# Attention scores by query: the spread operand moves from the keys to the queries, one head per matmul

## The reference

```
scores = einsum('bshd,bthd->bhst', q, k) * scale
attn   = softmax(scores + mask, axis=-1)
ctx    = einsum('bhst,bthd->bshd', attn, v)
```

## Time and profile before

| | |
|---|---|
| median of 3 runs | 1446.69 us (1445.44 to 1448.8) |
| span of the profiled execution | 1445.6 us |
| PE busy | 1301.3 us, 12165 matmuls and as many weight loads |
| DVE, POOL, ACT busy | 863.6, 702.4, 571.2 us |
| mean granted clock of PE | 0.961 of full speed |

### The profile page before, as it was taken

How to read it: one execution, slowest core, us unless ns; L and a number is a source line. 1 busy time by engine, 2 the same in 40 slices (tenths; PEclk the granted TensorE clock), 3 DMA queues, 4 the chain that set the end, 5 groups by cost and what they waited for, 6 DMA issues and landing times.

```text
span 1445.6 us, 33878 instructions
## 1 busy us (share of the span) xinstructions
PE 1301.3 (90%) x12165; PEld 1048.3 (73%) x12165; DVE 863.6 (60%) x2071; ACT 571.2 (40%) x1272; POOL 702.4 (49%) x949
## 2 busy tenths in 40 slices
PE   5998889989999999989999999959998999929887
PEld 4666647976777777767899899846766777628776
DVE  3788853337888888736622111258885778773346
ACT  1555545433444555643222222214443455414331
POOL 4566642017777466630233333237785555427426
PEclk9999989998999999979999999979999999959999
DMA  6000000020000000000389998631000000038954
GB/s 255 2 2 0 1 1 30 1 86 17 14 15 5 2 17 15 16 16 1 131 317 325 334 332 316 233 139 31 0 17 9 24 30 22 17 105 303 312 176 145
DMA packets 47371, 137.79 MB, mean 95 GB/s; under 512 B 6926, under 2 KB 29647, under 8 KB 41105
## 3 DMA queue, kind: packets, MB, share of 16 engines
q1 hardware_dynamic: 32944, 110.37, 21.7%
q0 software_dynamic: 7536, 19.67, 4.4%
q10 hardware_dynamic: 6768, 6.16, 1.2%
HBM read 119.54 MB, written 17.56 MB: 95 GB/s over the span
## 4 chain that ended last, share of the span: by engine, by line
PE 70%; DVE 12%; DMA 8%; issue 5%; POOL 3%; ACT 2%; DVEq 0%; SPq 0%; POOLq 0%; ACTq 0%
PE ps L1114 11%; PE ps L981 9%; PE ps L1032 9%; PE ps L1349 8%; PE ps L1076 6%; PE ps L1056 4%; PE ps L1047 4%; PE ps L1361 4%; DMA row_in<-rows_of,from_u 4%; DMA back_of<-w_odd 3%; PE ps L925 2%; PE ps L972 2%; DVE negmax L1791 2%; PE ps L1083 2%; PE ps L1007 2%
## 5 line engine op out<-in xcount | busy, mean ns | idle before, releaser
L1415 ACT ACTIVATE probsT_all<-ps 128x1024 f32<-128x1024 f32 x128 | 131.1, 1025 | 164.0 <-PE ps L981 164.0
L1791 DVE TENSOR_REDUCE negmax<-ps 128x8 f32<-128x1024 f32 x128 | 156.0, 1219 | 59.4 <-PE ps L981 59.2
L1349 PE MATMUL ps<-hT,w_tile 128*128 128x128 f32 x1304 | 161.9, 278 | 0.6 <-ACT act_sb L1673 0.2
L1349 PEld LDWEIGHTS ps<-hT,w_tile 128*128 128x128 f32 x1304 | 153.3, 193 | 3.1 <-issue 0.8
L981 PE MATMUL ps<-qe,kf 32*128 32x256 f32 x1280 | 153.1, 387 | 0.0
L981 PE MATMUL ps<-ke,qf 32*128 32x256 f32 x1024 | 146.0, 403 | 0.0
L759 POOL TENSOR_SCALAR eps_sum<-mv 128x1 f32<-128x1 f32 x112 | 25.5, 228 | 199.1 <-DVE mv L1728 112.2
L981 PEld LDWEIGHTS ps<-qe,kf 32*128 32x128 f32 x1280 | 111.0, 188 | 4.8 <-issue 2.8
L1076 PE MATMUL ps<-probsT_all,va 128*32 128x128 f32 x2560 | 105.4, 283 | 7.6 <-ACT probsT_all L1415 4.4
L2354 DVE TENSOR_TENSOR h_in<-ps,act_sb 128x512 f32<-128x512 f32 x39 | 27.0, 692 | 140.0 <-PE ps L1349 140.0
L700 POOL DMA_INDIRECT back_of<-be,to_u x39 | 39.4, 1010 | 140.4 <-DVE be L2367 140.4
(11 more groups left out here) (288 smaller groups left out, 3350.9 us busy)
## 6 DMA issues: line engine op xcount, KB each, us to landing
w_tile<-in_w_f SPq DMA_DIRECT2D x29, 1536.0 KB, 7.5
w_tile<-in_w_f SPq DMA_DIRECT2D x47, 385.0 KB, 7.0
y_back<-in_w_f SPq DMA_DIRECT2D x10, 1536.0 KB
back_of<-w_odd ACTq DMA_DIRECT2D x47, 128.0 KB, 6.5
ctxT<-in_ctxT SPq DMA_DIRECT2D x32, 128.0 KB, 2.1
rows_of<-nv SPq DMA_DIRECT2D x32, 128.0 KB, 1.7
w_even<-in_w_att SPq DMA_DIRECT2D x3, 1024.0 KB, 7.2
y_back<-back_of SPq DMA_DIRECT2D x6, 512.0 KB, 5.7
```

The costliest lines, as they stand in the source:

```text
L1349: last = mm(ps[:, 2 * which + at.two, fc * P:(fc + 1) * P], w[:, col:col + P], rowT[:, at.two, c, :], start=c == 0, stop=c == KC - 1)
L1415: nc.scalar.activation(half_of(probsT_all, half), ps[:, 2:4].rearrange("p b n -> p (b n)"), ACT.Exp, scale=HD ** -0.5).then_inc(S["probs"], 1)
L1791: nc.vector.tensor_reduce(m, ps[:, 0:2].rearrange("p b (h k) -> p (b h) k", h=HB), AX.X, ALU.max, negate=True).then_inc(S["s_max"], 1)
```

## The change

The spread keys `ke` are dropped. The spread queries `qe`, which `by_key` needs anyway, serve `by_query` too: as stationary operand, one head at a time (128 columns), with the plain keys `kf` as moving operand (128 columns). POOL makes one spread copy for each tile instead of two. `by_query` waits for `qe_sb` where it waited for `ke_sb`, and what waited for `s_out` of two tiles back before it wrote `qf` again (ACT, DVE) waits for `qe_sb` of that tile.

```diff
@@ heads_apart on POOL
                 wait(pool, *(("rotated", tile) if tile.l in ROTARY else ("qk_sb", tile)))
-                wait(pool, "s_out", tile.back(2))
-                apart(ke[:, tile.p], kf[:, tile.q]).then_inc(S["ke_sb"], 1)
                 wait(pool, "st_out", tile.back(4))
                 apart(qe[:, tile.q], qf[:, tile.p]).then_inc(S["qe_sb"], 1)
@@ by_query on PE
-                p, q, last = tile.p, tile.q, tile.back(1)
+                q, last = tile.q, tile.back(1)
                 if half == 0:
-                    wait(pe, "ke_sb", tile)
+                    wait(pe, "qe_sb", tile)
...
-                return [(b, j, qf[:, p], ke[:, p], tile.l == ATT1, "s_out", half) for b, j in enumerate(strips(half, False))]
+                return [(b, j, qe[:, q], kf[:, q], tile.l == ATT1, "s_out", half) for b, j in enumerate(strips(half, False))]
@@ scores on PE
                 for c in range(KC):
-                    for bank, j, a, b, first, name, half in products:
-                        done[name, half] = mm(ps[:, bank, c * D:(c + 1) * D], a[strip(j), c], b[strip(j), c].rearrange("p i k -> p (i k)"),
-                                              start=first, stop=first or c == KC - 1)
+                    for i in range(2):
+                        for bank, j, a, b, first, name, half in products:
+                            if name == "s_out":
+                                at = c * D + i * P
+                                done[name, half] = mm(ps[:, bank, at:at + P], a[strip(j), c, i], b[strip(j), c],
+                                                      start=first, stop=first or c == KC - 1 and i == 1)
+                            elif i == 0:
+                                done[name, half] = mm(ps[:, bank, c * D:(c + 1) * D], a[strip(j), c],
+                                                      b[strip(j), c].rearrange("p i k -> p (i k)"),
+                                                      start=first, stop=first or c == KC - 1)
@@ queries_keys on ACT, before it writes qf and kf
-                    wait(act, "s_out", tile.back(2))
+                    wait(act, "qe_sb", tile.back(2))
@@ rotate on DVE
-                    if tile.l in SOFTMAX:
-                        wait(dve, "s_out", tile.back(2))
+                    wait(dve, "qe_sb", tile.back(2))
```

More of the change, by code:

```diff
@@ L160 @@
         "zmax_sb": (ATT0,), "zero_exp": (ATT0,), "pad_mask": (XATT0,), "pad_in": (XATT0,), "gn_var": (RET,),
-        "gn_eps": (RET,), "gn_rstd": (RET,), "ke_sb": SOFTMAX, "nm_sb": SOFTMAX, "m_out": SOFTMAX, "inj_sb": SOFTMAX,
+        "gn_eps": (RET,), "gn_rstd": (RET,), "nm_sb": SOFTMAX, "m_out": SOFTMAX, "inj_sb": SOFTMAX,
         "o_sb": (RET,), "rotated": ROTARY}
@@ L286, in build @@
             kf = at_attention("kf", [P, 4, KC, P])
-            ke = at_attention("ke", [P, 2, KC, 2, P])
             qe = at_attention("qe", [P, 4, KC, 2, P])
@@ L368, in sem @@
             return S[name]
-        for name in ("var1 rstd1 u_norm var2 rstd2 v_norm base_sb uT_out hT_sb qk_out v_out qk_sb swapped rotated o_sb centred qe_sb ke_sb va_sb "
+        for name in ("var1 rstd1 u_norm var2 rstd2 v_norm base_sb uT_out hT_sb qk_out v_out qk_sb swapped rotated o_sb centred qe_sb va_sb "
                      "s_out s_max st_out probs pv_out nm_sb m_out inj_sb zero_exp o_norm oT_out oT_sb y_out x_done "
```

## The result

The changed kernel takes 1432.76 us (median of 7 runs, 1428.86 to 1441.6) where the kernel before takes 1445.44 us on the same chip (7 runs, 1443.39 to 1448.8). The ratio is 0.9925, interval [0.9896, 0.9954]: faster by 12.7 us in the medians, by 6.6 to 15 us in the interval. The prediction was 1440.8 us, range 1436 to 1448. The three ratios amount to 10.8, 12.5 and 8.4 us.

The account below looks back on a forecast made before the run. PE bounds the kernel, busy nine tenths of the span, with DVE's chain deciding in ATT0. -3.6 - 0.8 + 0.4 - 1.0 - 0.8 - 0.3 + 0.2 = -5.9 us gives span 1439.7, median 1440.8 us; range 1436 to 1448.

Parts of the forecast that it names:

- Rival (a): Query strips in `scores`: narrow pairs outrun the cover of the keys, slower, 1523 us at the upper bound; chance 0.15.
- `s_out` comes 0.03 us later: ATT0: the queries' signal, heading DVE's chain once a step, comes 0.03 us later; 13 steps cost 0.4 us.
- 0.2 in the calls with queries alone: PE in `scores`: the 6 calls without key products end 0.03 us later each, costing 0.2 us together.
- POOL's direct work: POOL, all softmax layers: 64 copies of 1.05 us go, 67 of 702 us; directly worth nothing.
- -3.6, -0.8 and +0.4: ATT0: ten steps lose 0.36 us each (-3.6), an eleventh at 176.6 gains 0.8, the later `s_out` costs 0.4 us.
- (b): ATT0: gain not realised, POOL meets another DVE operation or PE's next wait takes it; about -1.5 us, 1445 us; chance 0.23.
- (c): ATT0: L849 too slips past L1814, PE's whole wait goes in ten steps; 3 us more, 1438 us; chance 0.08.
- The start of XATT0: XATT0's start: DVE's wait for the rstd behind POOL's `ke` and `qe` shortens without `ke`; -1.0 us.
- XATT1: -0.3 forecast: Where RET passes into XATT1: DVE's L1757, held 0.28 us by `qe` behind `ke`, is freed; -0.3 us.
- The two steps in which PE waited behind `ke`: Steps at 466.59 and 606.12: PE idles 0.48 and 0.35 us for maxima held by POOL, and gets it back; -0.8 us.
- The step that failed: Other steps of XATT0, ATT1 and XATT1: hold-ups shrink, but PE is never idle there; worth nothing.
- the cover: Mixed calls of `scores`: key strips start later and end the call, so queries done 0.03 us later cost PE nothing.

Follow-up runs that it names:

- Experiment 2: Changed kernel with POOL's spread copy of the keys left in ahead of `qe`, read by nobody; ratio to the kernel before 0.9991 [0.9965, 1.0017].
- Experiment 4: Changed kernel with POOL's unread key copy kept in one layer only; ratio to the kernel before 0.9988 for ATT0 alone, 1.0004 for XATT0 alone.
- experiment 5: Changed kernel with the tensor `ke` still laid out in SBUF, neither written nor read; ratio to the kernel before 0.9954 [0.9921, 0.9987].
- experiment 3: Changed kernel with POOL's unread key copy as the last instruction of POOL's step; ratio to the kernel before 1.003 [1.0007, 1.0052].
- norm_next: Changed kernel with POOL's L846 moved in ATT0 into the next step, behind `inj`; 1427.1 us, ratio to the kernel before 0.9914 [0.9881, 0.9948].

## Why the prediction came out as it did

**PE: right on the pace, wrong on the signal.** Pace 0.112 us, queries 1.16 us from the call's start, keys last at 1.24, as much as before. Rival (a) didn't come in its time: no matmul started late behind a wide one. But its thought, queries held up behind keys, holds for the semaphore: the term "`s_out` comes 0.03 us later" measures 0.17 us, and the maxima of half 1 start 0.18 us later in ATT0 (4.02 instead of 3.84 us into the step). Where nothing else sets the pace, this is a price of the change: the second step of ATT0, ahead of the norm work on POOL, goes from 9.99 to 10.16 us, and three steps of XATT1 by 0.18 us each (13.48 to 13.66, 9.46 to 9.64, 9.11 to 9.29), the same in both profiles of before and in all eleven of PE's new form, with POOL's copy or without it. The maxima start 0.17 to 0.18 us later in each of these steps too. With 0.4 us in ATT1 (steps 2, 7, 14, 15) that is 1.1 us, where the forecast had 0.4 in ATT0 and 0.2 in the calls with queries alone.

The rule of the Trainium skill that was weighed (page "TensorE: Matmul & The Clock Gate", section "The mechanism", a load overlaps only matmuls of another row group) would, by the prediction's estimate, have made the changed kernel 82 us slower; 0.9925 and the row of 1.16 us for sixteen pairs on two strips contradict it.

**POOL's direct work: right.** POOL is at 638.2 us (forecast 635). Experiment 2 shows that the whole gain comes through it.

**ATT0: mechanism right, size too big.** -3.6, -0.8 and +0.4 made -4.0; -2.8 was measured over the same steps. A usual step lost 0.29, not 0.36 us (the ten of the forecast 2.3 us together, the eleventh its 0.8 us). From the start of the maxima to the end of the cuts VectorE's chain is 0.44 us shorter (2.77 instead of 3.21), but it starts 0.18 us later. What ends late in it is the one cut that L846 (L849 before) still holds (L1810 in 6 steps, L1818 in 7): L846 starts some 0.28 us after ScalarE's `fT_hi` has ended and so could move up by no more than 0.31 us (5.56 instead of 5.87 us into the step). By these figures the late signal costs nothing extra in these steps; no run takes it away. Rivals (b) and (c) are both refuted by the 11.06 us.

**The start of XATT0: -1.0 forecast, -0.6 measured. XATT1: -0.3 forecast, +0.3 measured.** The forecast term itself came: the first step goes from 10.51 to 10.23 us, and POOL's copy (experiment 2) takes it back to 10.51. The three steps with the late signal outweigh it. **The two steps in which PE waited behind `ke`: -0.8 forecast, -1.7 measured** (9.95 to 9.29 us around 466.59, 10.38 to 9.39 us around 606.12).

**The step that failed** is the last of the part on POOL: "In the other steps of XATT0, ATT1 and XATT1 the same hold-ups shrink, but PE is never idle there, and they are worth nothing." For ATT1 and XATT1 it holds: their other steps are as long as before, or longer by the late signal. In XATT0 it fails: besides the 0.7 us of the step at 466.59, its steps are worth 1.5 to 1.9 us, where the forecast had nothing. PE had hardly any idle time there that the list of waits shows, but it had slack within its busy time. A step of XATT0 before: POOL's second copy, the second cut that it holds, `inj`; then PE's padding matmuls, the first score matmul of the queries, the `inj` matmuls and the first of the keys.

```profile
382.06 1.04 POOL L778 TENSOR_TENSOR qe<-qf,const 128x512 f32<-128x512 f32 x1
382.17 0.96 DVE L1819 TENSOR_TENSOR nmx<-negmax,nmx 128x16 f32<-128x16 f32 x1
...
384.06 0.69 DVE L1834 TENSOR_TENSOR inj<-ps,const 128x512 bf16<-128x512 f32 x1
...
385.02 0.38 PE L981 MATMUL ps<-ke,qf 32*128 32x256 f32 x2
385.11 0.39 PE L972 MATMUL ps<-inj,ones_bf 32*128 32x512 bf16 x2
...
385.32 0.39 PE L981 MATMUL ps<-qe,kf 32*128 32x256 f32 x2
```

And the changed kernel:

```profile
373.99 0.18 DVE L1823 TENSOR_TENSOR nmx<-negmax,nmx 128x16 f32<-128x16 f32 x1
...
376.33 0.27 PE L981 MATMUL ps<-kf,qe 32*128 32x128 f32 x2
376.34 0.38 PE L969 MATMUL ps<-inj,ones_bf 32*128 32x512 bf16 x2
...
376.55 0.37 PE L984 MATMUL ps<-qe,kf 32*128 32x256 f32 x1
```

Before, the keys start 0.30 us after the queries, after the change 0.22. The keys end the call, so 0.08 to 0.1 us of a usual step is two strips running while the other two wait for `inj`: PE counts as busy, and the step is 9.12 instead of 9.01 us (median). Two of the steps won more, 0.45 and 0.28 us, which was not traced. The prediction itself had the fact that the key strips wait for `inj`, and used it for the cover only. Experiment 4 confirms the place: the copy in XATT0 alone takes these steps from 9.01 to a median of 9.29 us.

**The sum and the range.** By steps the change is worth about -6.1 us, against -5.9 forecast. That they agree is luck: an ATT0 1.2 us too big, a start of XATT0 0.4 us too big and a late signal priced too low nearly cancel against an XATT0 and an ATT1 priced too low. Yet the medians differ by 12.7 us. The other 6.6 are in no term of the prediction. Single executions of one kernel scatter by 5 to 13 us on this chip (7 of each kernel; by up to 23 us over the 27 of before on the last one), of which the range, drawn from the terms' own bounds, took no account: with them 1436 was too high an edge. A profile pair can mislead in the same way: this one differs by 15.5 us, and 4.6 of them are that the profiled execution of before begins later than its repeat (37.8 against 33.2 us to the first exponential), which goes with the clock (last section), not with the change. What stays open is a remainder of some 2 to 6 us beyond the steps, which all three ratios show (8.4, 10.8 and 12.5 us), though each interval but that of the second chip reaches down to 6.6 us or less. One candidate is seen: where ATT1 ends and MoE's gate begins, the execution is either short or some 4 to 5 us longer with the lower clock. All four profiles with the changed kernel's instructions (experiment 5's among them) are short, before is once long and once short, and five of the seven others are long. In the thirteen profiles the stretch from ATT1's last exponential to XATT1's first is 463.5 to 470.2 us in the short case and 470.8 to 475.9 us in the long one. The granted clock from 605 to 640 us (third number from the end), before and after:

```profile
605.00:640.00 35.00, 30.02 (x273) 21.27 (x273) 17.48 (x37) 17.27 (x36) 16.40 (x22) 0.81 0.05 17
```

```profile
605.00:640.00 35.00, 29.89 (x246) 22.48 (x246) 16.39 (x37) 17.54 (x38) 12.34 (x18) 1.00 0.05 17
```

Whether the change makes the short case likelier, or four of four is chance, no run tells apart.

## What to carry to other kernels

A small VectorE operation that takes several times its shortest time and ends just after one of GpSimd's is a cost that can be moved: ask not how busy GpSimd is, but which stretch of VectorE's queue has no slack, and place GpSimd's work behind its end (a copy in the wrong place costs 0.8 us a step in experiment 3, 11.84 against 11.06; L846 in the right one gives 0.4). An engine without idle time still gains from an earlier input when its array works in strips of which some wait; compare the start of the first matmul on each strip before pricing a wait at nothing. A matmul that ends early need not tell its reader early: look when the reader starts, not when the matmul ends. In norm_next, where L846 no longer sets the end of the cuts, VectorE's chain still begins at 4.02 us, so the 0.15 us by which the signal trails its matmul are worth about 2 us over 13 steps (an estimate from these figures; no run puts the last query matmul ahead of the last key matmul in the program). And before a profile pair is subtracted, take a second profile of each: steps repeat to 0.1 us, starts and stage ends don't.

## What the runs showed of the hardware

**The clock at the start is a matter of the execution.** The same 16 matmuls of the first projection, with the same work before them, in before and in the changed kernel:

```profile
19.61 3.78 PE L1032 MATMUL ps<-hT,w_even 128*128 128x128 f32 x16 [1.51 <-ACT hT L1408]
```

```profile
19.28 2.05 PE L1036 MATMUL ps<-hT,w_even 128*128 128x128 f32 x16 [1.71 <-ACT hT L1412]
```

The execution of before gets full speed at about 36 us, its repeat at 23.4, all eleven profiles of the changed and edited kernels between 17 and 24. The two executions that differ by 13 us there differ by 4.6 us in the first exponential.

**Time goes with the mean clock.** Over the 209 executions that entered comparisons on the chips, least squares with one slope for all and a level for each kernel and chip give 6.6 us (standard error 0.5) for 0.01 of mean granted clock; single executions of before lie between 0.948 and 0.971 on one chip. This is an association; no run sets the clock, and the mean counts the time ahead of the first record as full speed, so it leaves the start out. At equal clock the changed kernel is 10.8 and 8.6 us ahead on the two later chips (standard error 1.3 and 1.0), so the remainder named above is still in it.

**Strips start in their own order, but signal in the program's.** In the changed kernel the query matmuls with index `i == 1` of a chunk stand behind the wide key matmuls in PE's program, and none started late for them: their starts keep the pace of 0.112 us. But the semaphore of the last one rises 0.06 us after that of the keys in all 122 mixed calls, even in XATT0, where its own matmul has ended 0.28 us before; in the kernel before, with the queries ahead of the keys in the program, it rises 0.12 us (0.22 in XATT0) before that of the keys. The ends of matmuls in the trace are modelled, the semaphore events are recorded, and the readers' starts agree with the events.
